# Six of eight trees by leaf-row fetch, with two buffers of normalised rows, in a fused ViT tower

## What is computed

```python
h = patches @ tok_W.T + tok_b                       # 768 -> 256
# gated attention on layernorm(h)
x  = layernorm(h); xn = x / max(rms(x), eps) * g
uv = silu(xn @ uv_w.T)                              # u, v: 512 each, base: 128
q, k = rope(base * gamma + beta)
kernel = square(relu((q @ k.T + w_rel) / sqrt(128)))
h = h + x * res_scale + (u * (kernel @ v)) @ o_w.T
# eight binary decision trees of depth 7 on layernorm(h)
logits = x2 @ W_in.T + b_in                         # 8 trees x 255 nodes
# in each tree the token walks from the root: right where the node's logit > 0
out = (silu(logits) * on_path) @ W_out.T
h = h + out
```

## Time and profile before

| | |
|---|---|
| time, median of 3 runs | 2026.34 us (2025.54 to 2026.86) |
| the profiled execution: time / span | 2028.2 us / 2026.4 us |
| PE busy | 1973.2 us, 97% |
| DVE busy | 1702.8 us, 84% |
| ACT busy | 1397.2 us, 69% |
| POOL busy | 1001.6 us, 49% |
| mean DMA rate | 80 GB/s |
| indirect fetches on POOL | 512 |

### The profile page before, as it was taken

The page is one execution under the profiler, slowest core; times in us unless marked ns, Lnnn a source line. Parts: engine busy times, 40 slices in busy tenths (PEclk is TensorE's granted clock), DMA queues, the critical chain, the costliest instruction groups (busy, mean ns, idle before and its releaser), DMA issues. The chain is left out here.

```text
span 2026.4 us, 41146 instructions
## 1 busy us (share of the span) xinstructions
PE 1973.2 (97%) x12488; PEld 1858.1 (92%) x12488; DVE 1702.8 (84%) x4210; ACT 1397.2 (69%) x3085; POOL 1001.6 (49%) x1001
## 2 busy tenths in 40 slices
PE   6799999999999999999999999999999999999997
PEld 5689999999999999999999999999999999999986
DVE  5598888898888898888898888898888898888875
ACT  5467776677776676776676776676776776776764
POOL 2675445545445545445545545545545545545544
PEclk8999999999999999999999999999999999999999
DMA  4423223223222223223233223232223233222222
GB/s 131 108 75 93 76 77 82 79 72 90 77 75 81 78 76 87 74 77 80 75 83 84 75 76 82 73 86 83 75 75 81 74 87 83 75 75 79 61 68 80
DMA packets 81999, 163.12 MB, mean 80 GB/s; under 512 B 17102, under 2 KB 48048, under 8 KB 81968
## 3 DMA queue, kind: packets, MB, share of 16 engines
q0 software_dynamic: 40960, 103.02, 19.3%
q1 hardware_dynamic: 41008, 59.71, 10.3%
HBM read 148.76 MB, written 13.90 MB: 80 GB/s over the span
## 5 line engine op out<-in xcount | busy, mean ns | idle before, releaser
L483 POOL DMA_INDIRECT leaf_rows<-leaf_table,leaf_at x512 | 582.2, 1137 | 156.0 <-issue 156.0
L861 DVE TENSOR_TENSOR hid_lo<-hid,hid_hi 128x392 fp32r<-128x392 f32 (+1 forms) x256 | 255.3, 997 | 77.3 <-ACT hid_hi L551 77.2
L1168 PE MATMUL out_acc<-hid_hi,outw_lo 128*128 128x392 f32 x768 | 300.3, 391 | 0.2 <-DVE hid_lo L861 0.2
L456 POOL TENSOR_TENSOR inv_root<-to_root,minus_half 98x8 f32<-98x8 f32 x64 | 95.7, 1495 | 412.7 <-DVE to_root L911 266.1
L1168 PE MATMUL hid_ps<-ffn_x,in_lo 128*128 128x392 f32 x768 | 272.1, 354 | 1.8 <-ACT hid L706 0.7
L1170 PE MATMUL out_acc<-hid_hi,outw_hi 128*128 128x392 f32 x768 | 263.4, 343 | 0.0
L1169 PE MATMUL hid_ps<-ffn_x,in_hi 128*128 128x392 f32 x768 | 262.8, 342 | 0.0
L1169 PE MATMUL out_acc<-hid_lo,outw_hi 128*128 128x392 f32 x768 | 262.2, 341 | 0.0
L1170 PE MATMUL hid_ps<-ffn_x,in_hi 128*128 128x392 f32 x768 | 261.4, 340 | 0.0
L496 POOL TENSOR_TENSOR row_sum<-leaf_rows,row_sum 98x1024 f32<-98x1024 f32 x96 | 221.3, 2305 | 40.3 <-ACT leaf_rows L743 34.6
L482 POOL TENSOR_TENSOR held<-minus_half 98x1 f32<-98x1 f32 x128 | 35.7, 279 | 373.6 <-ACT v_full L637 199.6
(11 more groups left out here) (142 smaller groups left out, 5854.6 us busy)
## 6 DMA issues: line engine op xcount, KB each, us to landing
x_raw<-x SPq DMA_DIRECT2D x192, 196.0 KB, 2.4
out<-out_stage SPq DMA_DIRECT2D x32, 392.0 KB
leaf_rows<-leaf_table,leaf_at POOLq DMA_INDIRECT x512
leaf_table<-leaf_rows SPq DMA_DIRECT2D x4, 256.5 KB, 4.2
out_stage<-in_w SPq DMA_DIRECT2D x4, 256.0 KB
tok_major<-tok_w SPq DMA_DIRECT2D x3, 256.0 KB, 4.3
late_raw<-out_w SPq DMA_DIRECT2D x6, 128.0 KB
u<-uv_w SPq DMA_DIRECT2D x1, 576.0 KB, 4.2
```

Source lines behind the costliest of these rows:

```text
L483: pool.indirect_dma_start(row_slot(s, g), None, table, bass.IndirectOffsetOnAxis(ap=leaf_at[:, s, g:g + 1], axis=0), element_offset=s * P ...
L861: dve.tensor_tensor(out, src, hi.bitcast(F32), ALU.subtract).then_inc(done, 1)
L1168: pe.matmul(out, w[1], x_parts[0], start=start, stop=False)
```

## The change

- `GATHERED` is 6 instead of 4: trees 4 and 5 are also done by inner half, leaf number and fetched row; trees 6 and 7 stay dense. The slots stay eight.
- `leaf_x` gets a second buffer; `normed2` is a list of two, and `norm_apply`, `turn_ffn_x` and `leaf_dots` are told which to use. `norm_apply(n, 1, .)` waits for the dots of the unit two before.
- The loop runs two units per turn (step 2, two bodies), since the buffer is chosen when the code is written.
- All four hand-written orders are new, and the bodies' cut moved: dots, scaling, fetches and sums of trees 2 to 5 now reach over into the next body (`p`).
- At the start six trees' leaf weights are turned and stored instead of four, and two fewer dense pieces are loaded and split.

```diff
-GATHERED = 4
+GATHERED = 6
-        leaf_x = sb("leaf_x", [P, GROUPS * ROW_IN], F32)
+        leaf_x = sb("leaf_x", [P, 2, GROUPS * ROW_IN], F32)
-                        pool.wait_ge(rows_summed, SUMS * i + s + 1 - TREES_HELD)
+                        pool.wait_ge(rows_summed, SUMS * i + s + 1 + TREES_HELD - GATHERED)
-                    if which == 1 and not first(n):
-                        act.wait_ge(dotted, GROUPS * GATHERED * n)
+                    if which == 1 and not (isinstance(n, int) and n < 2):
+                        act.wait_ge(dotted, GROUPS * GATHERED * (n - 1))
-            with pool.Fori(2, UNITS - 2) as i:
-                body(i - 1, i, i + 1, i + 2)
+            with pool.Fori(2, UNITS - 2, 2) as i:
+                body(i - 1, i, i + 1, i + 2, 1, 0)
+                body(i, i + 1, i + 2, i + 3, 0, 1)
```

More of the change, by code:

```diff
@@ L575, in copy_h, with norm_apply @@
                                bias=c(COL_TOK_B + m)).then_inc(h_ok, 1)
[L577 removed]
+            def norm_apply(n, which, g, side):
                 if n is None:
@@ L1074, in uv_low, with body @@
                     low(uv_part(uv_lo, m, at), raw, uv_part(uv_hi, m, at), front_w_lo)
-            def body(p, i, n, nx):
+            def body(p, i, n, nx, a, b):
+                decisions(p, 7)
+                leaf_dots(p, 4, a)
+                hid_low(p, 6)
+                ffn_x_low(i, 0)
+                ffn_x_low(i, 1)
+                mask(p, 7)
                 norm_stats(n, 0, 0)
@@ L1120, in body @@
                 kern_low(n, 1)
-                x_low(nx, 1)
                 hid_low(i, 4)
+                decisions(i, 6)
+                leaf_dots(i, 2, b)
                 gate(n, 0)
@@ L1130, in body @@
                 gate(n, 3)
+                x_low(nx, 2)
                 mix_low(n, 3)
-                leaf_dots(i, 2)
-                mask(i, 6)
                 update_h(n, 0)
+                leaf_dots(i, 3, b)
                 update_h(n, 1)
-                decisions(i, 7)
-                x_low(nx, 2)
+                x_low(nx, 3)
                 norm_stats(n, 1, 0)
@@ L1417, in turn_rows, with body @@
                     last.then_inc(rows_turned, 1)
-            def body(p, i, n, nx):
+            def body(p, i, n, nx, a, b):
+                tree_visits(p, 2)
+                turn_normed(i, 0)
+                turn_normed(i, 1)
+                make_base(i)
+                make_v(i, 0)
+                if first(i):
+                    turn_rows()
+                tree_logits(p, 4, 0)
+                find_leaf(p, 2)
+                tree_out(p, 0, 0)
+                tree_out(p, 0, 1)
+                tree_visits(p, 3)
+                tree_out(p, 1, 0)
+                tree_out(p, 1, 1)
+                make_v(i, 1)
+                make_v(i, 2)
+                tree_visits(p, 4)
+                tree_logits(p, 5, 0)
+                find_leaf(p, 3)
+                make_v(i, 3)
                 make_u(i, 0)
-                tree_visits(p, 4)
-                tree_logits(p, 5, 1)
+                tree_out(p, 2, 0)
+                tree_out(p, 2, 1)
+                make_u(i, 1)
+                find_leaf(p, 4)
                 scores(i, 0)
-                make_u(i, 1)
                 tree_logits(p, 6, 0)
+                tree_visits(p, 5)
                 scores(i, 1)
-                tree_visits(p, 5)
                 make_u(i, 2)
                 tree_logits(p, 6, 1)
+                tree_out(p, 3, 0)
                 make_u(i, 3)
-                tree_out(p, 3, 0)
                 mix(i, 0)
@@ L1434, in body @@
                 mix(i, 2)
+                find_leaf(p, 5)
+                tree_visits(p, 6)
                 mix(i, 3)
-                tree_visits(p, 6)
                 tree_out(p, 3, 1)
-                tree_logits(p, 7, 0)
+                embed(n, 0)
                 project_o(i, 0, range(0, 3))
@@ L1461, in body @@
+                tree_visits(i, 0)
+                tree_out(p, 6, 1)
                 tree_logits(i, 1, 0)
-                tree_visits(i, 0)
-                tree_out(p, 6, 0)
                 tree_logits(i, 2, 0)
+                tree_visits(i, 1)
                 find_leaf(i, 0)
-                if first(n):
-                    turn_rows()
-                tree_visits(i, 1)
-                tree_out(p, 6, 1)
                 tree_logits(i, 3, 0)
+                find_leaf(i, 1)
                 add_rows(p)
@@ L1472, in body @@
                 tree_out(p, 7, 0)
-                tree_out(p, 7, 1)
                 turn_xn(n, 0)
                 turn_xn(n, 1)
-                tree_logits(i, 4, 0)
-                find_leaf(i, 1)
-                tree_out(i, 0, 0)
-                tree_out(i, 0, 1)
-                turn_normed(n, 0)
-                tree_visits(i, 2)
-                tree_out(i, 1, 0)
-                turn_normed(n, 1)
-                make_base(n)
-                make_v(n, 0)
-                tree_visits(i, 3)
```

322 lines of the change are left out of this document (163 added, 159 removed).

## The result

The changed kernel takes 2290.75 us (median of 4 runs, 2286.14 to 2294.09) where the kernel before takes 2026.44 beside it. The ratio is 1.130, with a 95% interval of 1.129 to 1.132. I had forecast 2046 us in a range of 1955 to 2105: the sign was right, and the size was off by 245 us. PE has 11980 matmuls; I had worked out 11976.

What follows compares the result with a forecast made beforehand. The prediction took PE alone to bound the steady state. Four segments of 9.5 + 2.3 + 12.4 + 37.4 = 61.6 us against 60.93 gave +20 us over some 30 units: 2046 us, range 1955 to 2105.

Steps and rivals of the forecast that it cites:

- PE's own work: PE's matmul work per unit, all else hidden: falls from 60.9 to 57.15 us.
- the whole step of 0.65: Change in length of a whole unit, 60.93 to 61.6 us; for some 30 units +20 us.
- DVE's own work: DVE's busy time per unit: net +1.9 us, from 52.7 to 54.6 of 57.15.
- POOL: POOL's fetches, sums and small `held` per unit: 17 us more, about 47, with gaps some 52 of 57.
- The rival in which POOL decides: POOL's chain up to `add_rows` sets the unit: 62.5 to 64.5 us, centre 63.5, 2104 us; chance 0.2.
- A: Segment from end of `project_o` to end of `embed(n, 5)`: 11.2 us before, 9.5 after.
- B: Segment from end of `embed(n, 5)` to `turn_h(n, 0)`: 1.40 us before, 2.3 after, PE standing still for 1.4.
- C: Segment from `turn_h(n, 0)` to `turn_xn`: 11.9 us before, 12.4 after, DVE in series; end above 13.8.
- a third of the collision: Share taken for `sum_rows(p, 4)` meeting the moments between `turn_h` and `turn_xn`; the whole was up to 1.8 us.
- D: Segment from `turn_xn` to end of `project_o`: 36.5 us before, 37.4 after; end above 38.7.
- The loop: Turn of the two-unit loop: costs nothing visible, as PE's order shows no gap where a turn begins.
- DVE's series and the port: Serial DVE work with one collision of two-SBUF-operand instructions and POOL sums decides: unit 61.1 to 62.5 us; chance 0.36.

Runs made afterwards that it cites:

- run 5: Changed kernel as straight code, with `sum_rows` adding 1 of 256 columns and the rest of the sum left out: 2019.07 us, 0.996.
- small sums: `sum_rows` adds 1 of 256 columns, the rest left out: 2020.96 us in the kernel before, 2019.07 in the straight code, 2087.47 in the changed kernel with its loop.
- run 9: Straight code with two memsets of about a sum's length together ahead of each sum over 1 column, the rest of the sum left out: 2106.14 us, 1.039.
- run 8: Kernel before, with four idle ACT copies between the two `copy_h` of each unit of the loop, so that PE rests: 2070.10 us, 1.0215.
- run 4: Changed kernel with its loop, plus 12, 14 and 14 spare matmuls into unread columns ahead of three PE rests: 2245.09 us, 1.108.
- straight code: Changed kernel with its four compute loops written out, so no loop turn stands between units: 2265.19 us, 1.118.
- run 7: Straight code plus 14, 14 and 22 spare matmuls into unused columns where PE rests: 2210.68 us, 1.091.
- run 12: Changed kernel with its loop of two units, each row sum over 1 of 256 columns, the rest left out: 2087.47 us, 1.029.

## Why the forecast was wrong

By the steps of its own:

- **PE's own work, right.** 57.86 us busy a unit in run 5 against 57.15. The 0.7 us are small beside the loss, but as large as the whole step of 0.65 that I forecast.
- **DVE's own work, right in the step, wrong in the base.** The 52.7 us a unit of before had 3 us of held time in them. With small sums in both kernels DVE is busy 1612 us before and 1662 after, 1.6 us more a unit, where the step said 1.9. But the held time grew from 3 to 8 us a unit (6 in the loop), and it came on top: DVE's 59.8 of 67.98.
- **POOL, right.** About 51 of busy time and gaps (42.81 and 24 gaps of 0.34) against "some 52". The rival in which POOL decides isn't what happened: its sign was `add_rows` waiting for `sum_rows(p, 5)`, and PE waits there once in the whole run. POOL's own time costs at most about 87 us (run 9).
- **A and B, right** (9.43 and 2.39). B's wait costs its length (run 8).
- **C, a collision mis-sized.** 14.39 where I took 12.4: "a third of the collision" was a mean over chances. Units repeat, so a collision comes in nearly all of them or in nearly none. This one came in 28 of 32, with 2.7 us where my end above had 1.8, as the step was held from within the fetch on.
- **D, the term that failed most.** 41.77 where I took 37.4 and had an end of 38.7. The held `leaf_dots(i, 2)` was in the walk, at 1.4 us; it is held 1.8 and makes PE wait 1.6 at `mix`. What wasn't there is what comes of it: the clock, 39.47 - 36.10 = 3.4 us of PE in D.
- **The clock stood nowhere in the sum.** The kernel before showed 1.00 in its steady state, with a PE that never rested, so no row of it had a price. But I had forecast a rest a unit, and collisions that would make others, and should have asked. It is worth at least 46 us in the changed kernel (run 4) and 54 in the straight code (run 7).
- **The loop, taken at nothing.** "There is no gap in PE's order where a turn begins" is true of a body of one unit. The page showed 16 and 15 packets of instructions for 30 units, which says that this body isn't fetched again; it says nothing of twice as much code. It costs 25 us here, 32 in the kernel before, 68 with small sums.

The sum by what was measured: from 2026 to 2019 without sums and loop (a unit 0.5 us shorter, 15 us, less about 8 of start and end), +246 for the sums, +25 for the loop: 2290. In the other order it is +68 for the loop (run 12) and +203 for the sums, so the two aren't separate costs. Of the 246 some 54 at least are the clock (run 7), and some 159 go with the two-operand hold, the clock's part among them (run 9). What POOL's length costs without any hold on DVE stays open, between 0 and about 87 us, as every form of POOL work that I had still holds one kind of DVE instruction.

The range failed for one reason behind these: both its ends came from a unit in which each effect stands alone. The hold on DVE makes PE rest, and behind some of these rests the clock falls. Of the forecast, the sign came out by the way that was foreseen (DVE's series and the port), but the +20 us had neither the clock nor the loop in it.

## What to carry to other kernels

Slack on the engine behind the bound is what makes its collisions free: the kernel before had 100 us of held DVE time and paid 5, and a change that spends this slack can pay for all of them at once, so count the held time of before as a debt, not as part of the work. In a loop a collision tends to be there in nearly every turn (28 of 32 here) or in hardly any; take it whole or leave it. Where a change gives PE rests that it did not have, put a possible fall of the clock into the upper end of the range. Before a loop's body is doubled, look at the packets of instructions: few of them for many turns means that the body stays loaded, and a longer one may not.

## What the runs showed of the hardware that I had not expected

- A `TENSOR_SCALAR` of four columns with one SBUF operand is held by POOL's fetch and sum (2.90 us) and by fetch and memset (2.51), against 0.16 to 0.17 alone. My rule in the forecast had only two-operand instructions. The Trainium skill's "SBUF — State Buffer", section "Who interferes with whom", says that `tensor_scalar` can enter a mode that takes both ports, when its operands meet the conditions, and that the engine which comes second is then blocked for a whole instruction. The hold agrees with that, also beside a memset, which reads nothing; that the mode was entered no run shows. I had read past it.
- The clock of TensorE fell to 1.2 GHz with three rests of 1.4 to 2.6 us a unit (mean clock 0.931, straight code), and with one or two of 1.5 to 2.4 us in run 12 (0.965). It didn't with one rest of 1.5 a unit (0.991), one of 1.38 (1.00 between 400 and 800 us in run 5), or five of up to 1.5 (run 7, 1.00 over the unit from 1000 us). Which rest it falls behind stays open.
- At a turn of the loop of two units PE or DVE stands 2.0 to 2.4 us with no releaser, where the loop of one unit showed no such wait. In time a turn costs 1.8 us in the changed kernel, 2.3 in the kernel before and 4.9 with small sums (25.6, 32 and 68 us over 14 turns).
